# Adjacency stage of a graph network: run-time tables read into registers eight values at a time, one load ahead

## The reference, cut to what matters

```python
h = jax.ops.segment_sum(h[src], dst, num_segments=3125)   # five times in _appnp, twice more in _gin
```

## Time and profile before

| what | value |
|---|---|
| median of 3 runs | 4482.73 us (4481.22 to 4483.88) |
| the profiled execution's own time | 4474.41 us |
| its span, first to last instruction | 4472.6 us |
| busy: PE, DVE, ACT, POOL | 3216.3, 2593.4, 1319.4, 2122.7 us |
| the adjacency stage | from about 736 to about 1016 us of the span |

### The profile page before, as it was taken

One profiled execution on the slowest core, in us unless ns is written; L12 is line 12 of the kernel. 1 busy time (PEld: TensorE's weight loads), 2 busy tenths in 40 slices (PEclk: granted clock), 3 DMA queues, 4 the chain that ended last, 5 costly groups with the idle time before them and its releaser, 6 DMA issues. The chain is left out here.

```text
span 4472.6 us, 76205 instructions
## 1 busy us (share of the span) xinstructions
PE 3216.3 (72%) x18744; PEld 2222.9 (50%) x18758; DVE 2593.4 (58%) x9443; ACT 1319.4 (29%) x2922; POOL 2122.7 (47%) x2166
## 2 busy tenths in 40 slices
PE   2588854666999999479999679999555555555553
PEld 1366642224666666357777457777333333233332
DVE  7687884885555543658888657777632222522223
ACT  0188863750111100135555435555310000100000
POOL 0577770000000000357777257777357777077774
PEclk7598986987999999679999889999755555755555
DMA  2122212000000000266666254445111112422223
GB/s 57 40 72 71 74 61 80 1 1 22 17 16 17 17 13 15 75 169 180 182 178 177 52 149 127 131 130 124 27 55 53 53 53 52 145 53 53 53 53 62
DMA packets 257837, 330.87 MB, mean 74 GB/s; under 512 B 79104, under 2 KB 170063, under 8 KB 256271
## 3 DMA queue, kind: packets, MB, share of 16 engines
q1 hardware_dynamic: 189258, 209.96, 15.3%
q0 software_dynamic: 68256, 117.02, 11.9%
HBM read 232.30 MB, written 94.47 MB: 73 GB/s over the span
## 5 line engine op out<-in xcount | busy, mean ns | idle before, releaser
L2448 PE MATMUL gat_acc<-gat_rows,gat_hot 128*128 128x128 f32 x1664 | 576.2, 479 | 484.4 <-issue 246.7
L925 PE MATMUL hop_p_a<-hop_h,adj 128*128 128x384 bf16 x4375 | 726.2, 328 | 27.8 <-DVE hop_h L866 27.8
L2448 PEld LDWEIGHTS gat_acc<-gat_rows,gat_hot 128*128 128x128 f32 x1664 | 401.0, 316 | 660.8 <-issue 660.0
L925 PEld LDWEIGHTS hop_p_a<-hop_h,adj 128*128 (+1 forms) x4375 | 429.7, 98 | 317.3 <-DVE hop_h L866 35.6
L2432 POOL DMA_INDIRECT gat_rows<-typed_rows,gat_idx x416 | 394.2, 948 | 233.3 <-DVE gat_idx L2455 106.8
L1858 POOL DMA_INDIRECT lb_far<-far_rows,lb_idx x416 | 402.6, 968 | 195.3 <-issue 119.8
L2432 POOL DMA_INDIRECT gat_rows<-hidden_rows,gat_idx x416 | 395.0, 950 | 196.7 <-PE gat_acc L2448 81.1
L1858 POOL DMA_INDIRECT la_far<-far_rows,la_idx x416 | 409.3, 984 | 154.4 <-issue 117.7
L1591 POOL DMA_INDIRECT by_src_records<-scatter_rec,scatter_rank x375 | 381.9, 1018 | 129.1 <-issue 100.9
L2463 DVE TENSOR_SCALAR gat_hot<-iota_row,gat_tabs 128x128 f32<-128x128 f32 x416 | 147.9, 364 | 369.6 <-PE gat_acc L2448 363.9
L534 POOL DMA_INDIRECT mid_by_src_tab_rec<-by_src_records,by_src_off x4 | 4.0, 1002 | 736.6 <-POOLq L81 735.7
(11 more groups left out here) (503 smaller groups left out, 6426.2 us busy)
## 6 DMA issues: line engine op xcount, KB each, us to landing
edge_features<-emb_out SPq DMA_DIRECT2D x104, 256.0 KB
la_feat<-edge_features SPq DMA_DIRECT2D x104, 256.0 KB
edge_features<-la_out SPq DMA_DIRECT2D x104, 256.0 KB
lb_feat<-edge_features SPq DMA_DIRECT2D x104, 256.0 KB
la_place<-dst_row SPq DMA_DIRECT2D x104, 128.0 KB
lb_place<-dst_row SPq DMA_DIRECT2D x104, 128.0 KB
typed_rows<-typed_np_row SPq DMA_DIRECT2D x25, 512.0 KB, 2.6
hop_side<-x0share_nodes SPq DMA_DIRECT2D x125, 64.0 KB
```

The lines of the kernel that those rows point to most:

```text
L925: ins = nc.tensor.matmul(p_a[(u.par + r) % 2][:, 0:3 * D], K.adj[:, s, bass.ds(u.t * P, P)], h3[r % 2][:, s, :, :].rearrange("p i d -> p ( ...
L2448: nc.tensor.matmul(acc[:, bass.ds(at[u % LOADS], D)], hot[u % HOTS][:, :], rows[u % RING][:, :], start=False, stop=True, skip_group_check= ...
```

## The change

LOADS becomes 8, and each of the three queues keeps two sets of registers. The first load is issued before the loop; at each eighth unit (or cell) the queue takes over the set loaded earlier and issues the load of the next eight, in front of the eight waits at hand.

```diff
-    LOADS = 16
+    LOADS = 8
...
+            def cells_of(u):
+                _, cell = nc.values_load_multi_w_load_instructions(
+                    unit_cell[0:1, u:min(u + LOADS, UC)], engines=[mybir.EngineType.SP], min_val=1, max_val=CELLS)
+                return cell
+            ahead = cells_of(0)
             for u in range(UC):
                 if u % LOADS == 0:
-                    _, cell = nc.values_load_multi_w_load_instructions(
-                        unit_cell[0:1, u:min(u + LOADS, UC)], engines=[mybir.EngineType.SP], min_val=1, max_val=CELLS)
+                    cell = ahead
+                    if u + LOADS < UC:
+                        ahead = cells_of(u + LOADS)
                 sp.wait_ge(s_zero, cell[u % LOADS])
                 sp.sem_inc(s_free, 1)
```

More of the change, by code:

```diff
@@ L1115, in _, with ends_of @@
             pool.wait_ge(s_tab, 64)
+            def ends_of(c):
+                _, end = nc.values_load_multi_w_load_instructions(
+                    cell_end[0:1, c:min(c + LOADS, CELLS)], engines=[mybir.EngineType.Pool], min_val=AHEAD,
+                    max_val=UC + AHEAD)
+                return end
+            ahead = ends_of(0)
             for c in range(CELLS):
                 if c % LOADS == 0:
-                    _, end = nc.values_load_multi_w_load_instructions(
-                        cell_end[0:1, c:min(c + LOADS, CELLS)], engines=[mybir.EngineType.Pool], min_val=AHEAD,
-                        max_val=UC + AHEAD)
+                    end = ahead
+                    if c + LOADS < CELLS:
+                        ahead = ends_of(c + LOADS)
                 pool.wait_ge(s_unit, end[c % LOADS])
@@ L1134, in _, with wins_of @@
             pe.wait_ge(s_tab, 64)
+            def wins_of(u):
+                _, win = nc.values_load_multi_w_load_instructions(
+                    unit_win[0:1, u:min(u + LOADS, UC)], engines=[mybir.EngineType.PE], min_val=0,
+                    max_val=(WINS - 1) * WIN, skip_runtime_bounds_check_because=BOUNDED)
+                return win
+            ahead = wins_of(0)
             for u in range(UC):
@@ L1137, in _ @@
                 if u % LOADS == 0:
-                    _, win = nc.values_load_multi_w_load_instructions(
-                        unit_win[0:1, u:min(u + LOADS, UC)], engines=[mybir.EngineType.PE], min_val=0,
-                        max_val=(WINS - 1) * WIN, skip_runtime_bounds_check_because=BOUNDED)
+                    win = ahead
+                    if u + LOADS < UC:
+                        ahead = wins_of(u + LOADS)
                 if k == 0:
```

## The result

The changed kernel takes 4441.44 us (median of 6 runs, 4439.45 to 4444.23); the kernel before 4481.71 us (6 runs, 4471.96 to 4483.88). The ratio is 0.9912, 95% interval 0.989 to 0.9935: 0.9% faster, clear of the 0.2% that can be told from no change. I had forecast 4456.5 us with a range from 4447 to 4471; the gain came out at about 40 us where I had worked out 26.

What follows compares the result with a forecast made beforehand. DVE was taken to set the stage's pace, losing 37.5 us waiting for PE. Without the start's 3.2, 34.3 - 5 - 3 = 26.3 us saved; 4482.7 - 26.3 = 4456.4, say 4456.5 us, range 4447 to 4471.

Steps and rivals of the forecast that it cites:

- one load ahead: On each in-order queue, loads and checks only move eight units earlier, still between two waits; saves nothing.
- the start keeps its 3.2 us: DVE's first wait stays 3.2 us, since each queue does two loads of eight there instead of one of sixteen.
- SP's load of eight: On SP's queue, loading eight values takes 0.52 us, from 0.97 us for sixteen times PE's ratio 0.53.
- the upper bound of 0.76: Longest time taken for SP's load of eight, 0.76 us, from POOL's single value of 512 ns plus a slope.
- SP's capacity: SP's queue needs 3.19 us per eight units against DVE's 3.28, so it keeps up with 0.09 us to spare.
- the 17 waits in the middle with 28.8 us: DVE's waits for PE between the first and the last; all 28.8 us were to go.
- 0.25 us for each of POOL's 21 freezes, 5 us: Loss kept each time POOL's queue gives nothing out during load and checks: 5 us (between 0 and 14).
- The last stall: DVE's last wait, 5.45 us, behind PE's 4.52 us wait at 972.86; 3 us were taken to remain.
- rival 1: SP's load of eight stays 0.97 us, so SP is the bound at 3.64 us a set; 4469 us, chance 0.06.
- 4: SP's queue: load of eight at 1.01 us with gap, 47.0 us waits kept: 36 us more, 4519 us; chance 0.04.
- rival 2: POOL, ACT and SP delays coincide oftener, about 0.8 us each time, keeping 17 us; 4466 us, chance 0.16.
- rival 3: Nothing changes: SP's 47.0 us of waits for ACT's zeros stay, loads add 4 us; 4487 us, chance 0.08.

Runs made afterwards that it cites:

- order-only kernel: Changed kernel with LOADS back at 16, so the load ahead without smaller sets; 4489.0 us, ratio 1.0002 to the kernel before.
- the one with the second load: Changed kernel with one more, unread load of eight values on SP per set; the trace has no such load; stage 248.6 us.
- size-only kernel: Kernel before with LOADS = 8 and no load ahead; 4445.93 us, ratio 0.9909.
- four comparisons: Kernel before against changed kernel (two chips), sets of eight alone, sets of 4, 4, then 8: medians differ 3.9, 1.9, 2.5, -0.4 us more than stages.

## Why the prediction was wrong, step by step

**What held.** That the stage is DVE's, and that the 37.5 us of its waits, with what a wait costs beyond its length, are all that the queues hold back. That one load ahead "hides nothing": shown by the order-only kernel. That the start keeps its 3.2 us: it kept 3.3, and loses most of it once the load ahead is gone. SP's load of eight: 0.52 us forecast, 0.523 measured; the pair of sizes on PE was the right row to go by, the upper bound of 0.76 was not needed. SP's loads of one and of four values took 266 and 297 ns. The Trainium skill (page "DMA: Bandwidth & Descriptors", section on latency and other measured facts) states a floor of about 600 ns; these register loads from SBUF are under it, and the measurement decides. SP's capacity: 3.19 us for eight units forecast; measured from the first to the last load, without the 5.3 us of waits for ACT, (974.4 - 742.4 - 5.3) / 71 = 3.19. That the 17 waits in the middle with 28.8 us go: they went.

**What failed, first.** The step "I put that at 0.25 us for each of POOL's 21 freezes, 5 us". The measured value is 0, in three executions (the changed kernel twice, and the one with the second load). The step had PE's lateness creep up to the 1.4 us that DVE bears and charged every freeze of POOL with what went beyond; but the lateness never got that far, since PE's longest wait for SP behind the start was 1.30 us. It put a steady loss where there is a threshold. With POOL's freeze left at 5.1 us and SP's halved, 8.3 us were left for 10 such freezes of POOL, 0.8 us each; with both halved, none. In the changed kernel SP waited for ACT 10 times and 5.3 us in all, where it had been 47 times and 47.0 us, so that the lateness behind POOL's freezes hardly reached SP's releases. Why it did not is only argued: SP, at 3.19 of 3.28 us, seldom gets as far ahead as the seven banks allow, and PE, no longer at the lower clock behind long waits, makes up for a small lateness sooner. No run takes the two apart.

**Second.** The step "*The last stall* ... I take 3 us". PE's wait at this place fell from 4.52 us to 1.30:

```profile
938.53 1.52 PE L1163 MATMUL adj_acc<-adj_hot_dst,adj_hot_src 128*128 128x512 bf16 x6 [1.30 <-SPq L1115]
```

That is 3.2 us less, where SP's own freeze accounts for 2.48; it stayed below the 1.4 us that DVE bears, and DVE did not wait. The step subtracted the 2.48 us from DVE's wait instead of from PE's: 4.52 - 2.48 leaves PE 2.0 us, and less the 1.4 us that DVE bears, 0.6. The size-only kernel shows just this, one set further on: PE waits 2.00 us and DVE 0.60.

```profile
945.21 1.96 PE L1145 MATMUL adj_acc<-adj_hot_dst,adj_hot_src 128*128 128x512 bf16 x8 [2.00 <-SPq L1109]
```

Without the two steps the sum was 34.3 us.

**Third, a term that was not in the sum.** A DVE wait costs more than its length. Around the wait of 2.93 us that ends at 800.89 the groups start at

```profile
795.83 0.82 DVE L1173 TENSOR_TENSOR adj_hot_src<-adj_iota,adj_src 128x640 bf16<-128x640 f16 x1
...
803.03 0.82 DVE L1173 TENSOR_TENSOR adj_hot_src<-adj_iota,adj_src 128x640 bf16<-128x640 f16 x1
```

so the group with the wait takes 5.06 - 2.93 = 2.13 us and the next 2.14, where others take 2.05. All 19 waits before show the first, nine of them the second as well. From DVE's first group to its last it comes to this (the last two times of each row):

```profile
L1173 DVE TENSOR_TENSOR adj_hot_src<-adj_iota,adj_src x114: 807/816/826, 741.0 to 1012.5; 128x640 bf16<-128x640 f16 x114
```

```profile
L1191 DVE TENSOR_TENSOR adj_hot_src<-adj_iota,adj_src x114: 804/806/826, 742.9 to 977.9; 128x640 bf16<-128x640 f16 x114
```

271.5 us before and 235.0 after, 36.5 less, of which the waits are 34.2. The other 2.3 us are 0.13 for each of the 18 waits that went. They are the 36.4 - 34.3 = 2.1 us by which the stage gained more than the sum over the waits, but for 0.2 us by which the changed kernel is later at its start.

**The rest of the miss.** 8.0 us of the two steps and 2.1 of the third bring 4456.5 to 4446.4. The median of before in the second series was 1.0 us under the one that I started from. The last 4 us (4445.4 to 4441.4) are within the interval of the ratio, about 10 us to each side, and lie outside the stage, where four comparisons showed no steady difference.

**The rivals.** The load of eight did shrink (rival 1, and with it 4). The sum of rival 1 was off as well: it counts the 57 sets from 748 to 974 us, but SP feeds DVE over all 71, so 26 us would be lost and 4474 us come out, above my range. POOL, ACT and SP in a row kept nothing rather than half (rival 2): with one of the two freezes left whole they would have kept a quarter to 40%. Nothing changes (rival 3) asked for SP's 47.0 us of waits to stay; they fell to 5.3. What went wrong was my leaning towards rival 2 after working out a full gain: all of the 34.3 us was the bound of my range with one us beyond it, and it was the likeliest case by the sum over the waits. The range was too narrow on that side, since it left out the restart of DVE and the spread of the rest of the program. Of the signs, the numbers and lengths of the loads came as said; DVE's waits came to 3.3 us and not 11, ACT's longest wait for POOL inside the stage to 1.6 us and not 1, and PE's waits for SP in the middle to 29 in 57 sets, not one in each.

## What to carry to other kernels

A load of registers with its checks is work on an in-order queue, and issuing it earlier on the same queue hid nothing here; what counts is how long the queue gives nothing out at a time, against the lead and the buffers of those that it feeds. Halving that time can remove a stall entirely, so a stall should be compared with its threshold and not scaled. From the other side the queue's capacity limits how small a set may be: here eight was within 3% of the pace of the busiest engine, four was just over it, and two and one were slower than the kernel before.

## What the runs showed of the hardware that was not expected

- A register load from SBUF on SP took 266 ns for one value, 468 for two, 297 for four, 523 for eight, 747 for twelve and 971 for sixteen. Two values cost more than four. On POOL one value took 287 ns in the sets of one, where the lone load at 62.5 us that the prediction took for its upper bound had 512.
- The check of a value against its bounds takes 0.253 us of SP's queue (two instructions), more than four times the 0.056 us that one more value adds to a load of eight or more. Leaving the checks out was not tried.
- Two chips differed by 930 us on the same kernel, and by the barriers nearly all of it lies in five stages in which POOL issues indirect transfers (L1591, L1858 and L2432 among them), while the stage of the change, which has no transfers but its tables, agreed within 0.6 us. Why was not looked into.
